# A four-layer sequence model on one core: q·k sums of the differential attention on TensorE, LoRA's q and k in fp32 strips, expert tables in one transfer

## The reference

```python
# L0: causal attention, 8 heads of 16, with a rank-one term; then 8 experts 128->512->128, each token to one
# L1: differential attention ACROSS the 32 half-heads of ONE token (q, k of depth 4), then FF 512, then MX-quantised linear
att = einsum('bnqd,bnkd->bnqk', q, k)          # q, k: [token, 32, 4]; att: [token, 32, 32]
att = softmax(nan_to_num(att)); att2 = att[first halves] - lam * att[second halves]    # [token, 16, 16]
out = rmsnorm(einsum('bnah,bhnd->bnad', att2, v)) * (1 - LAMBDA_INIT)                  # v: [token, 16, 8]
# L2: LoRA attention: 16 heads of 8, not causal, W + A.B/16; then 14 experts 128->256->128
y = x @ W.T + x @ A.T @ B.T * SCALING ;  softmax(q k^T / sqrt(8)) v
# L3: causal attention, 16 heads, q and k of depth 128 ("wide"), v of depth 8; then 8 experts 128->128->128
```

## Time and profile before

| | |
|---|---|
| runs, median (lowest, highest) | 3064.21 us (3063.6, 3069.54), 3 runs |
| profiled execution | 3066.79 us, span of the core 3065.6 us |
| PE, DVE, ACT, POOL busy | 2069.4, 1719.4, 1144.4, 658.3 us |
| prologue / EARLY / EARLY+MID | 69.6 / 231.0 / 308.6 us |
| six passes of all three | 337.2, 338.1, 335.3, 337.5, 339.5, 334.2 us |
| MID+LATE / LATE | 278.5 / 156.1 us |

### The profile page before, as it was taken

One profiled execution on the slowest core, in us unless ns is written; L12 is line 12 of the kernel. 1 busy time (PEld: TensorE's weight loads), 2 busy tenths in 40 slices (PEclk: granted clock), 3 DMA queues, 4 the chain that ended last, 5 costly groups with the idle time before them and its releaser, 6 DMA issues. The chain is left out here.

```text
span 3065.6 us, 42852 instructions
## 1 busy us (share of the span) xinstructions
PE 2069.4 (68%) x13457; PEld 1422.5 (46%) x13457; DVE 1719.4 (56%) x4319; ACT 1144.4 (37%) x2744; POOL 658.3 (21%) x904
## 2 busy tenths in 40 slices
PE   3530757487956796588857796569748795569483
PEld 3330433355544563456444564447435554345352
DVE  2346636565774667465765677456756577452132
ACT  0320323254533462255434453336325452234251
POOL 2015012400251113400250014210350025200101
PEclk9775875698868895699778895789679886787695
DMA  6120040405041222304040413222140504111402
GB/s 172 44 67 4 7 126 0 113 1 126 22 119 38 69 65 75 97 12 121 26 138 9 101 32 104 68 52 81 43 130 1 126 21 117 37 22 29 139 1 58
DMA packets 263744, 200.39 MB, mean 65 GB/s; under 512 B 28708, under 2 KB 236964, under 8 KB 262980
## 3 DMA queue, kind: packets, MB, share of 16 engines
q1 hardware_dynamic: 257348, 184.77, 22.4%
q0 software_dynamic: 6144, 12.60, 1.4%
HBM read 151.18 MB, written 35.49 MB: 61 GB/s over the span
## 5 line engine op out<-in xcount | busy, mean ns | idle before, releaser
L1573 DVE TENSOR_REDUCE mid_room<-ps 128x2 f32<-128x512 f32 x256 | 164.0, 686 | 152.8 <-PE ps L911 149.9
L1168 ACT ACTIVATE late_room<-ps 128x384 f32<-128x384 f32 x256 | 125.6, 491 | 286.3 <-PE ps L849 283.4
L1214 ACT ACTIVATE mid_room<-ps 128x512 f32<-128x512 f32 x256 | 152.3, 598 | 142.1 <-PE ps L924 137.3
L1180 ACT ACTIVATE late_room<-ps,late_neg_max 128x128 f32<-128x128 f32 (+1 forms) x512 | 186.6, 419 | 46.7 <-DVE late_neg_max L1550 42.5
L1015 PE MATMUL ps<-mid_pool 128*128 128x128 f32 x544 | 123.7, 365 | 84.0 <-DMA mid_pool<-moe_small 50.9
L911 PE MATMUL ps<-mid_pool 48*128 48x256 bf16 x512 | 67.3, 296 | 146.3 <-DMA mid_pool<-mid_room 134.3
L924 PE MATMUL ps<-max_rows,of_unit 96*128 96x256 bf16 x512 | 164.6, 322 | 0.0
L1729 DVE TENSOR_TENSOR early_pool<-ps,early_pool 128x1024 f32<-128x1024 f32 x128 | 150.8, 1219 | 23.5 <-ACT early_pool L1270 16.3
L922 PE MATMUL ps<-mid_pool 48*128 48x256 bf16 x512 | 162.4, 317 | 0.5 <-ACT mid_room L1214 0.5
L839 PE MATMUL ps<-late_aT,heads_T 128*128 128x256 f32 x512 | 158.5, 392 | 0.0
L1252 ACT ACTIVATE mid_room<-ps,mid_pool 128x128 f32<-128x128 f32 x272 | 84.9, 364 | 181.5 <-PE ps L1015 181.2
(11 more groups left out here) (378 smaller groups left out, 5300.9 us busy)
## 6 DMA issues: line engine op xcount, KB each, us to landing
mid_pool<-in_m_w_dram SPq DMA_DIRECT2D x272, 128.0 KB, 2.1
early_pool<-m_folded_w SPq DMA_DIRECT2D x88, 256.0 KB, 3.2
early_pool<-in_m_w_dram SPq DMA_DIRECT2D x88, 256.0 KB, 3.2
mid_pool<-mid_room SPq DMA_DIRECT2D x192, 64.0 KB
heads_T<-in_m_w_dram SPq DMA_DIRECT2D x176, 64.0 KB
mid_pool<-moe_small SPq DMA_DIRECT2D x136, 65.0 KB, 1.9
mid_room<-moe_sorted_in SPq DMA_DIRECT2D x32, 256.0 KB, 3.0
moe_sorted_out<-mid_room SPq DMA_DIRECT2D x32, 256.0 KB
```

The costliest lines, as they stand in the source:

```text
L1168: act.activation(probs_T[s][:, k % (2 * QUAD), :], ps[:, s.last_bank, 0:3 * P], ACT.Copy)\
L1180: ins = act.activation(probs[s][:, n % RING, qt, 0:w], ps[:, bank, qt * P:qt * P + w], ACT.Exp, bias=neg_max[s][:, n % RING, qt:qt + 1])
L1214: act.activation(probs_T[s][:, n % (2 * QUAD), :], ps[:, B + slots.index(("unit", n)) % S_BANKS, :], ACT.Exp)\
L1573: dve.tensor_reduce(all_max[:, :, n], ps[:, B + n % S_BANKS, :].rearrange("p (q k) -> p q k", q=2), AX.X, ALU.max, negate=True).then_inc(s ...
```

## The change

1. **Differential attention.** DVE makes products for one depth index at a time (128x1024), and PE adds the four of them in PSUM with the identity as weights (`add_products`, two matmuls of 512 columns for each depth index); the clamp reads PSUM. The products with v are laid out by head, and PE adds the 16 heads (`add_values`, 16 matmuls of 128 columns a tile), ACT keeps the result. The eight DVE sums of a tile are gone. q, k and v are kept in SBUF in a ring of three.
2. **LoRA.** Projections are made by padded weights `lora_qk` so that each head lies on 9 rows of a 32-row strip: row 0 of k is one, row 0 of q is zero at first. There are 8 projection matmuls instead of 2, no bf16 parts, and no stacking DMAs. Scores are fp32 matmuls of 9 rows. After the maxima, q is projected again (4 matmuls) and the maxima, written as columns of `max_cols`, are added to row 0 of each strip by 16 transposing matmuls; `direct_scores` is then two fp32 matmuls a unit.
3. **Tables.** All parts of an expert's table lie together in DRAM (`whole`) and come by one DMA. The copies into `whole` for the 14 and the last 8 experts are issued by ACT in the prologue and waited for after the EARLY block.
4. **Order.** There are three strings, one each for EARLY+MID, MID+LATE and all three; steps and `DIFF_PARTS` have other counts. Some semaphores of the prologue are merged.

```diff
-LORA = Attention("lora", 16, 8, 2)
+LORA = Attention("lora", 16, 8, 8)
-BODY_ORDER = ( "LELLEMEMEEELMEEEEMEELEMEMEEM" ...
+ORDERS = { "EM": ( "EMEMEMEMEEMEEMEEEM" ... ), "ML": ( "LLMLMLMLMLMLLLLLLM" ... ), "EML": ( "LMLEEMLLEELMEELMEE" ... ) }
@@ sync: fetch_table
-                    sp.dma_start(tables[s][:, i, 0:m.w2_at], layer1[m][:, bass.ds(expert, 1), :]).then_inc(here, 16)
-                    sp.dma_start(tables[s][:, i, m.w2_at:m.b2_at],
-                                 layer2[m][:, bass.ds(expert * m.chunks, m.chunks), :]).then_inc(here, 16)
-                    sp.dma_start(tables[s][:, i, m.b2_at:m.width],
-                                 small[m][bass.ds(expert * P, P), :]).then_inc(here, 16)
+                    sp.dma_start(tables[s][:, i, :].unsqueeze(1), whole[m][:, bass.ds(expert, 1), :]).then_inc(here, 16)
@@ sync: mid
-                    for w, order in ((0, SPLIT_Q), (1, SPLIT_K)):
-                        sp.wait_ge(parts_ready, w + 1)
-                        for j, i in enumerate(order):
-                            for half in range(2):
...
-                                sp.dma_start( stacks[...], parts[...] ).then_inc(stacks_here, 16)
@@ scalar, prologue
+                act.wait_ge(weights_here, LOADED)
+                for dst, src in later_copies:
+                        act.dma_start(dst, src).then_inc(later_tables, 16)
@@ tensor: direct_attention
-                            pe.matmul(region, k_of(h)[:, at0 + kt * P:at0 + (kt + 1) * P],
-                                      q_of(h)[:, at0:at0 + SEQ_LEN], start=True, stop=False)
-                            mm = pe.matmul(region, of_unit[:, n:n + 1].broadcast_to([SPLITS * STRIP, P]),
-                                           max_rows[:, :], start=False, stop=True)
+                            mm = pe.matmul(region, k_of(h)[:, at0 + kt * P:at0 + (kt + 1) * P],
+                                           q_of(h)[:, at0:at0 + SEQ_LEN], start=True, stop=True)
...
-                    pe.wait_ge(stacks_here, 16 * 2 * 2 * len(SPLIT_Q))
+                    for b in range(at.blocks):
...
+                        pe.matmul(ps[:, B + b % S_BANKS, :], weight_of(b // half, b % half), aT[s][:, :],
+                                  start=True, stop=True).then_inc(sig("block_ready"), 1)
...
+                    for b in range(half):
...
+                        pe.matmul(bank, weight_of(0, b), aT[s][:, :], start=True, stop=False)
+                        for t in range(TILES):
+                            mm = pe.matmul(bank[:, t * P:(t + 1) * P], max_cols[:, b * TILES + t, :], ident[:, :],
+                                           start=False, stop=(t == TILES - 1))
@@ tensor: early
+                    def add_products(t, ds):
+                        for d in ds:
+                            pe.wait_ge(prod_ready, DIFF_D * t + d + 1)
+                            for half in range(2):
+                                mm = pe.matmul(ps[:, B + half, :], ident[:, :],
+                                               prod[:, d % 2, half * BANK:(half + 1) * BANK],
+                                               start=(d == 0), stop=(d == DIFF_D - 1))
+                            mm.then_inc(prod_used, 1)
+                    def add_values(t, half):
...
+                        for h in range(half * n, (half + 1) * n):
+                            mm = pe.matmul(ps[:, s.last_bank, 3 * DIM:], ident[:, :],
+                                           dprod[:, h, :, :].rearrange("p a e -> p (a e)"),
+                                           start=(h == 0), stop=(h == DIFF_HEADS - 1))
@@ vector: early
-                        for i in quarters:
-                            tick(dve.tensor_reduce(dscores[:, i * 256:(i + 1) * 256], prod[:, i % 2, :, :],
-                                                   AX.X, ALU.add))
-                        link(dve.tensor_scalar(dscores, dscores, FLT_MAX, -FLT_MAX, ALU.min, ALU.max))
+                        dve.wait_ge(prod_used, DIFF_D * (t + 1))
+                        link(dve.tensor_scalar(dscores, ps[:, B:B + 2, :].rearrange("p b n -> p (b n)"),
+                                               FLT_MAX, -FLT_MAX, ALU.min, ALU.max))
```

More of the change, by code:

```diff
@@ L91 @@
 TABLES = 4
-TABLE_DMAS = 3
 ROUND = 1.5 * 2.0**23
@@ L125 @@
 DIRECT_LAG = 2
-SPLITS = 3
+STRIPS = 4
 RING = 2
@@ L536, in _ @@
                 for b in range(WIDE_HALVES):
-                    sp.dma_start(wide_raw[:, b], a["wide_qk"][:, b]).then_inc(wide_raw_here[b], 16)
+                    sp.dma_start(wide_raw[:, b], a["wide_qk"][:, b]).then_inc(weights_here, 16)
                 for dst, src in loads:
                     sp.dma_start(dst, src).then_inc(weights_here, 16)
-                for dst, src in small_copies:
-                    with nc.allow_non_contiguous_dma(reason="columns of small tables, once"):
+                for dst, src in first_copies:
+                    with nc.allow_non_contiguous_dma(reason="columns of tables, once"):
                         sp.dma_start(dst, src).then_inc(small_built, 16)
@@ L589, in _ @@
                                         channel_multiplier=0))
-                for j in range(SPLITS):
-                    link(pool.affine_select(out=of_unit[:, :], in_=of_unit[:, :], compare_op=ALU.not_equal, fill=1.0,
-                                            base=-j * STRIP, pattern=[[-1, STRIP]], channel_multiplier=1))
+                settle()
+                for j in range(STRIPS):
+                    link(pool.memset(strip_first[STRIP * j:STRIP * j + 1, :], 1.0))
             @block.tensor
@@ L681, in take_steps @@
         def take_steps(streams, programs):
-            letters = [s.name[0].upper() for s in streams]
-            for k in [letters.index(c) for c in BODY_ORDER if c in letters]:
-                next(programs[k])
+            letters = "".join(s.name[0].upper() for s in streams)
+            order = ORDERS[letters] if len(streams) > 1 else letters * len(WEIGHTS[streams[0]])
+            for letter in order:
+                next(programs[letters.index(letter)])
             for program in programs:
@@ L1192, in direct_attention, with keep_block @@
                     yield
-                    for w, bank in enumerate((B + 1, B)):
-                        act.wait_ge(sig("block_ready"), w + 1)
-                        act.activation(parts[:, w, 0, :], ps[:, bank, :], ACT.Copy).then_inc(high_kept, 1)
-                        yield
-                    yield from steps(3)
-                    yield from steps(at.units // 2 + 2)
+                    half = at.blocks // 2
+                    def keep_block(b):
+                        act.wait_ge(sig("block_ready"), b + 1)
+                        bank = ps[:, B + b % S_BANKS, :]
+                        if half <= b < at.blocks:
+                            ins = act.activation(lora_k[:, b - half, :], bank, ACT.Identity, bias=strip_first[:, 0:1])
+                        else:
+                            ins = act.activation(lora_q[:, b % half, :], bank, ACT.Copy)
+                        ins.then_inc(sig("block_kept_act"), 1)
+                    for b in range(0, at.blocks, 2):
+                        keep_block(b)
+                        yield
+                    yield
+                    yield from steps(at.units // 2)
+                    for b in range(at.blocks, at.blocks + half, 2):
+                        keep_block(b)
+                        yield
                     slots = slots_of(at, DIRECT_LAG)
@@ L1561, in direct_attention @@
+                    for b in range(1, at.blocks, 2):
+                        keep_block(b)
+                        yield
                     keep_values(s, at, B)
                     yield
[L1563 to L1569 removed]
@@ L1584, in direct_attention @@
-                    settle()
-                    for part in (second, third):
-                        tick(dve.tensor_copy(max_rows[part, :], max_rest[part]))
-                    settle()
-                    tell(dve.tensor_tensor(max_rows[third, :], max_rest[third], max_rows[third, :],
-                                           ALU.subtract), sig("max_split"))
-                    yield
-                    yield
+                    for b in range(at.blocks + 1, at.blocks + half, 2):
+                        keep_block(b)
+                        yield
```

404 lines of the change are left out of this document (224 added, 180 removed).

## The result

| | runs, median (lowest, highest) | ratio to before, 95% interval |
|---|---|---|
| before | 3066.64 us (3063.6, 3069.54), 4 runs (one more than in the section on the time before) | |
| changed | 3396.22 us (3386.86, 3405.19), 4 runs | 1.1069 (1.1039 to 1.1098) |

The forecast was 3105 us with a range to 3260. The direction was right, the size was off by a factor of eight: +330 us instead of +38.

A forecast was written before the change was run, and what follows sets the result against it. PE was taken as the fullest engine, with no engine full. Blocks summed 3065.6 + 66 (six passes) + 0 - 6 - 17 - 8 + 6 = 3106.6, so 3105 us; range 2970 to 3260.

The forecast's parts named there:

- PE's work, +76 us at full clock: Loop pass: LoRA, sums of products and sums with v raise PE's work from 202 to about 278 us.
- Rival B: Loop's scores: strips run side by side, both 27.5 to 9 us each, -37 a pass, about 2883; chance 0.05.
- The dense first part, 7 + 181: Loop pass: lead-in 7 us, then 163.4 full us of PE work up to q's second projection, divided by 0.9: 181.
- The clock, "with PE fuller I keep 8 of it": Second scores: half clock cost 22 us a pass before; with PE fuller 8 of it stays, making the pass 348.
- Rival C: Second scores and EARLY's sums: PE stays at half clock, or weight loads show; 367 a pass, 3219 us; chance 0.13.
- DVE's product at 1.22: EARLY's tiles: DVE's product takes 1.22 us for a depth index, PE's sums 1.72, so PE sets the pace.
- The clamp, "some tenths": EARLY's tiles: a clamp that reads PSUM takes some tenths off DVE's saving of 29 us a pass, 27 net.
- MID's way to its experts, and the order strings, put at nothing: Loop: MID's output, norms and router with the rest of EARLY's sums, 42 us where it was 40; no string term.
- Experts 31: MID's 17 expert blocks in a loop pass: with one table DMA 1.8 us each instead of 2.3, 31 us.
- rival D: Experts' tables: the single DMA does not shorten the tails, landing being the pace; 3168 at worst, inside the forecast's range.
- EARLY alone, 0: EARLY's own block: each tile loses 7 us on DVE and gains 10.4 on PE; taken as 0, between -9 and +25.
- EARLY+MID -6, MID+LATE -17: The two-stream blocks: waits for stacks and tables go, PE work comes; -6 (-25 to +20) and -17 us (-40 to +10).

The follow-up runs named there:

- k_by_depth: The changed kernel with the weight columns of k laid out by depth, so DVE's product reads neighbouring k values: 3339.99 us.
- one_dma_tables: The kernel before with only the third part of the change, expert tables by one DMA: 3053.42 us, ratio 0.9948.
- new_lora_old_order: The kernel before with the one-transfer tables and the new LoRA attention, in the old order string: 3271.09 us.
- both_old_parts: The changed kernel with the differential and LoRA attention of before, leaving the one-transfer tables and the new order strings: 3239.01 us.
- old_diff: The changed kernel with the differential attention of before, everything else changed, order strings too: 3283.94 us.
- after_old_order_k: The changed kernel with all its parts in the old order string (one EARLY step merged), k laid out by depth: 3572.36 us.
- tables_after_x: The kernel before with one-transfer tables, their eight later copies issued by SP behind the first load of x: 3042.16 us, ratio 0.9914.

## Why the prediction was wrong, step by step

The loop was forecast at 348 us a pass. Its terms beside the pass from 1814.0, and the same stretches of the pass before (from 1284.5):

| | before | forecast | measured |
|---|---|---|---|
| up to the second scores | 166.7 | 7 + 181 | 179.6 |
| second scores, then MID's way to its experts | 60.2 + 48.8 | 61 + 8, 42 | 74.6 + 66.5 |
| MID's experts | 40.1 | 31 | 36.2 |
| gather and barrier | 19.4 | 18 | 23.0 |
| pass | 335.2 | 348 | 379.9 |

The two parts of the second row are read together, since the forecast drew the line between them at 1185.4, 10 us behind the last score of that pass. **This row is the step that failed**: 111 forecast for 109 before, and 141.1 measured. It holds 30 of the 32 us by which the pass was missed, and the forecast had three things wrong in it: the clock, the product's price, and the order strings, for which it had no term at all.

- **PE's work, +76 us at full clock.** Nearly right: 269 us of work in a pass for the 277 counted, 202 before. What I had too high are the 9-row scores: I counted 0.86 us for a unit, nothing hidden; two units took 1.14 together, 0.57 each with the tail. Rival B was half true in its mechanism, and its time wrong in sign.
- **The dense first part, 7 + 181.** It held, 8 us to the good: 179.6.
- **The clock, "with PE fuller I keep 8 of it".** This failed. PE was busy 93% of the second scores, and the clock was 0.72: 74.6 us for 49.9 full us of work (69.27 x 0.72), where the forecast had 69 for 54.9. I had made the clock a consequence of PE's fullness. The runs show that the low matmuls hold it down here: with 128 rows in the place of 9 it is 1.00, the stretch 56.6 and the kernel 155 us shorter. That is as much as half of the loss, but not half of its causes, since the kernel before pays for its clock there too (60.2 us at 0.82). Rival C named the place, and I argued it down by a stretch of equal fullness (1106 to 1126) in which 122 of 146 matmuls were 128 rows high. Its own sum was too low as well: I added 27 us for half clock, but 54.9 full us take 110 at clock 0.50, not 88.
- **DVE's product at 1.22.** The row L1729 was of another reading pattern: the product took 2.07, of that 0.77 for the stride and most of the rest beside POOL. 56 us of the loss are the stride (k_by_depth). I had counted -27 us of DVE a pass; DVE's busy time fell by 10.4 only (212.0 to 201.6).
- **The clamp, "some tenths".** The clamp's group in the kernel before, and in the changed one, where it reads PSUM:

```profile
L1743 DVE TENSOR_SCALAR early_pool<-early_pool 128x1024 f32<-128x1024 f32 x32 | 21.5, 671 | 1.0
```

```profile
L1827 DVE TENSOR_SCALAR early_pool<-ps 128x1024 f32<-128x1024 f32 x32 | 39.2, 1224 | 81.1 <-PE ps L1083 81.1
```

  0.55 us more for each tile, on the path between PE's sums and ACT's exponential.
- **MID's way to its experts, and the order strings, put at nothing.** The forecast took this way over from the kernel before, in its string, and gave the new strings no term. It took 66.5 us; with k by depth 60.3, with few sums 60.2 (60.6 to 64.1 in other passes), with high scores 59.5, so the clock of the scores is not in it, and PE's sums don't show. The string and the differential attention both are:

| MID's way to its experts, us | old string | new strings |
|---|---|---|
| old differential attention | 49 (one_dma_tables), 48 to 49 (new_lora_old_order) | 66 (both_old_parts), 66 (old_diff) |
| new, k by depth | 65 to 66 (after_old_order_k) | 60 to 62 (k_by_depth) |

  Either one alone adds 17 us and both together 11; the LoRA attention makes no difference where both versions ran (the lower left cell has the new one alone, and the merged step of EARLY). For the whole kernel it is alike: the new strings cost the old parts 186 us and save the new parts 232. Which steps do it stays open; moving MID's forward made it worse.
- **Experts 31.** 36.2, from 40.1. PE still waits 60.8 us for tables (L1035) in the whole kernel: the landing is the pace more than SP's issue, rival D, in part.
- **EARLY alone, 0.** +18.5, of that 8 by the stride (241.7 us with k by depth). The end of my range was +25.
- **EARLY+MID -6, MID+LATE -17.** +21.7 and +16.5. EARLY+MID takes 326.7 us with k by depth, and 308.7, nearly as before the change, with high rows too: the clock again. MID+LATE stays some 9 us longer than before even with both edits, and that stays open.
- **Prologue +6, LATE -8.** +11.0 and -2; the cause of the former was the one named (tables_after_x takes it back).

With full rows and k by depth a pass is 353.5 us, beside the 348 of the forecast, and that closeness is in part luck: it comes with 56.6 us for the second scores where 69 were forecast, and 59.5 for MID's way where 42 were. The direction came out right; of its reason, more work on a full PE, the dense first part shows 13 of the 45 us by which this pass grew.

## What to carry to other kernels

Before replacing one matmul by a lower one, look at the granted clock where it will stand: here 128 matmuls of 9 rows that overlap each other cost more in the second scores than 128-row matmuls that do not, while the first scores kept full clock with as many. If leaving work out changes nothing while an engine is 93% busy, read the clock before looking for another bound. Where low and high matmuls alternate, read their pace from start to start before blaming the clock. An order of steps is worth what it is worth with the parts that it was made for, so a change of it needs a term and a run of its own. And price a new elementwise instruction by a row of the same stride and the same memories (SBUF or PSUM on each operand), not of the same size.

## What was not expected of the hardware

- PE 93% busy in the second scores, with 128 MATMULs of 9 rows among 320: mean clock 0.72; with 128 rows in their place: 1.00 at 99%; 3340 and 3185 us for the whole kernel. But 128 MATMULs of 9 rows among 452, PE 100% busy: 1.00.
- bf16 matmuls of 256 columns at clock 1.00: one every 0.21 us where 64 and 128 rows alternate, every 0.11 where all have 128.
- fp32 products on DVE with both operands in SBUF: 1.22 us for 1024 elements, 1.99 with a step of four on one operand, and up to 2.02 (3.06 with the step) beside POOL, whose additions double too (1.63 to 3.35 for three). With one operand in PSUM: none of 192 above 1.226.
- Two units' 9-row fp32 matmuls on different strips take 1.14 us where 128 rows take 1.89.
